# Row maxima and weight maxima of an attention kernel: over GpSimd and TensorE, or over VectorE's block transposes

## The chip, the core and the metric

The program runs on one core of a Trainium2 chip. The metric is the device time of one execution in microseconds, the median over several runs. Lower is better.

## The reference

A macaron block over x of shape 8 x 512 x 128 in float32: a feed-forward stage, an attention, and the same feed-forward stage again, each on a layer norm of x and added to x (the feed-forward stages with a factor 0.5).

```python
def attn(x, Q, K, VO):                                 # 16 heads, rank 64, dim 128
    xq = einsum('btd,hrd->bthr', x, Q)
    xk = einsum('bud,hrd->buhr', x, K)
    attn = softmax(einsum('bthr,buhr->bthu', xq, xk) / sqrt(128), axis=3)
    return einsum('bthu,bud,hde->bte', attn, x, VO)

def ffn(x):                                            # three blocks
    h = x
    for blk in range(3):
        y = qlora_linear(h, 2 * blk)                   # 4-bit weights, scales, bias, low-rank part
        y = gelu(layernorm(y, gamma[blk], beta[blk]))
        h = qlora_linear(y, 2 * blk + 1) + h
    return h

x = x + 0.5 * ffn(layernorm(x))
x = x + attn(layernorm(x), Q, K, VO)
x = x + 0.5 * ffn(layernorm(x))
```

## The kernel before, in words

Each engine has its own hand-written instruction stream, and the streams are tied by semaphores. There is no planner: the order on an engine is the order in the code.

**Feed-forward stage** (`ffn(f)` on each engine). Twelve units (three blocks of four units, a unit being two batches) go through a pipeline of steps i. On TensorE, step i holds the first linear layer of unit i (`lin1`, L899 and L902), the second of unit i - 3 (`lin2`, L919) and the turn of z of unit i - 2 (`turn_z`, L912). ScalarE makes squares (L441) and the gelu (L449); VectorE makes the seed of the reciprocal root (`seed`, L694 and L695), scales z (`z_scaled`, L703) and adds to h (`step_h`, L710); GpSimd runs three Newton steps of twelve small instructions on each unit's variances (`newton`, L333 to L336). Each batch has a PSUM bank of its own.

Beside the first of these stages the attention weights are prepared for a split into two fp16 halves. VectorE takes each partition's absolute maximum of Q, K and VO in steps 2, 3 and 5 and clamps it (`weight_maxima`, L616 to L621). After Newton step 5 GpSimd reduces these over all partitions with `partition_all_reduce` (L355). In step 7 VectorE makes powers of two and their inverses (`weight_scales`, L626 to L633). ScalarE makes the halves from step 7 on (`weight_halves`, L458 to L471), GpSimd the low halves after its last Newton step (L358, L360).

**Attention.** 128 heads (8 batches of 16) go through a pipeline of slots k, in a loop of four slots per turn, with the first and last ones written out. Heads are projected in pairs, since a head has 64 rows. What the engines do for head k or those near it in one slot:

- TensorE: scores of head k + 1 (`scores`, L986 and L987, eight matmuls of 512 columns); in even slots the turn of the row maxima of the pair k + 2, k + 3 (`turn_max`, L979); outputs of head k - 1 (`outputs`, L1008 to L1010, twelve of 128 columns); weighted sums of head k (`weigh`, L996 to L998, twelve of 512); a first product of queries and keys for the maxima of a pair ahead (`maxima`, L973, four of 512, 64 rows each); in odd slots the projections of queries and keys of a pair (`project`, L965 to L967, six of 512).
- ScalarE: exponentials of head k + 1 (`exps`, L522), their fp16 high half (`p_high`, L527), the high halves of a pair's queries and keys in odd slots (L514, L518), and the high half of y (L532).
- VectorE: in even slots the copy of the turned maxima of a pair into the score operands (`row_max`, L786); reciprocal and scaling of the outputs (`scale_out`, L795 and L799); two reductions of the maxima (`reduce_max`, L780, into `mcol`); in odd slots the low halves of queries and keys (L769, L774); the low half of y (`y_low`, L790).
- GpSimd: the low half of the exponentials (`p_low`, L375, two), and the addition of a head's output to x (L381).
- SyncE: ten DMAs per pair that spread the halves into `head_ops`, once the scores of the pair that used that place are done (`spread`, L260 to L271).

The row maximum reaches the scores as one more row of the product: row 64 or 96 of q2 holds minus the maximum, and the same row of k2 holds a one and zeros.

PSUM: banks 0 to 3 hold scores and maxima, bank 4 y, bank 5 the projected queries and, in other slots, the turned maxima, bank 7 the projected keys, and banks 6 and 7 the outputs, so that keys and outputs wait for each other.

Of the kernel before, what the change touches and what calls it, by code (L numbers as in the profile page):

```python
# [19 lines left out]
RMAX = bass.bass_isa.ReduceOp.max  # L20


def macaron(nc, x_d, q_d, k_d, vo_d, qw_d, sc_d, bias_d, la_d, lb_d, gam_d, bet_d, out_d):
# [14 lines left out]
    STEPS = NB * UNITS  # L38
    LN_EPS = 1e-5
# [7 lines left out]
    with ctx:  # L47
# [9 lines left out]
        ident16 = sb("ident16", [128, 128], F16)  # L57
# [22 lines left out]
        inv2 = sb("inv2", [128, 4])  # L80
        exp_scale = sb("exp_scale", [128, 1])
# [36 lines left out]
        mcol = sb("mcol", [128, 2, TT, 128], F16)  # L118
        M_ROWS = slice(R, R + 64, 32)
# [15 lines left out]
        qj_ps = ps[:, 5, :]  # L135
        kj_ps = ps[:, 7, :]
# [17 lines left out]
        prep_p = sem("prep_p")  # L154
        vo_folded = sem("vo_folded")
# [33 lines left out]
        m_turned = sem("m_turned")  # L189
# [13 lines left out]
        late_ps = ps[:, 6, :]  # L203

# [99 lines left out]
        def _(pool):  # L304
# [10 lines left out]
            pool.memset(mcol[:, :, :, :], 0.0).then_inc(prep_p, 1)  # L315
# [5 lines left out]
            pool.memset(head_ops[64:65, 0:RING:2, 3, :], 1.0).then_inc(prep_p, 1)  # L321
            pool.memset(head_ops[96:97, 1:RING:2, 3, :], 1.0).then_inc(prep_p, 1)
# [34 lines left out]
            pool.wait_ge(prep_p, 9)  # L357
# [54 lines left out]
        def _(act):  # L412
# [5 lines left out]
            nc.scalar.activation(ident_b[:, :], ident[:, :], ACT.Copy)  # L418
            nc.scalar.activation(ident16[:, :], ident[:, :], ACT.Copy).then_inc(prep_a, 1)
# [92 lines left out]
            def q_high(pair, buf):  # L512
                act.wait_ge(q_proj, pair + 1)
                nc.scalar.activation(pair_ops[:, buf, 0, :], qj_ps, ACT.Copy).then_inc(qh_ready, 1)  # L514

            def k_high(pair, buf):
                act.wait_ge(k_proj, pair + 1)
                nc.scalar.activation(pair_ops[:, buf, 2, :], kj_ps, ACT.Copy).then_inc(kh_ready, 1)  # L518
# [21 lines left out]
            def slot(k, j, lo, hi):  # L540
# [12 lines left out]
                if j % 2 == 1 and hi + 5 < NH:  # L553
                    turn = k // 4 if quad[0] is None else quad[0]
                    pair = 2 * turn + ((j + 5) // 2)
                    if lo + 5 >= 4:
                        pair_free(pair, ((j + 5) // 2) % 2, turn + (j + 5) // 4)
                    q_high(pair, ((j + 5) // 2) % 2)
                    k_high(pair, ((j + 5) // 2) % 2)
# [9 lines left out]
            for k in range(-5, 4):  # L569
# [25 lines left out]
        def _(dve):  # L595
# [130 lines left out]
            def ffn(f):  # L726
# [7 lines left out]
                for i in range(STEPS + 3):  # L734
                    if i >= 3 and i < STEPS + 2:
# [10 lines left out]
                    if f == 0 and i == 7:  # L746
                        weight_scales()
# [19 lines left out]
            def q_low(pair, buf):  # L767
                dve.wait_ge(qh_ready, pair + 1)
                nc.vector.tensor_tensor(pair_ops[:, buf, 1, :], qj_ps, pair_ops[:, buf, 0, :],  # L769
                                        ALU.subtract).then_inc(ql_ready, 1)  # L770

            def k_low(pair, buf):
                dve.wait_ge(kh_ready, pair + 1)
                nc.vector.tensor_tensor(pair_ops[:, buf, 3, :], kj_ps, pair_ops[:, buf, 2, :],  # L774
                                        ALU.subtract).then_inc(kl_ready, 1)

            def reduce_max(unit, par, t):

                dve.wait_ge(max_mm, unit + 1)
                nc.vector.tensor_reduce(mcol[:, par, t, M_ROWS], s_ps[t % 2], AX.X, ALU.max,  # L780
                                        negate=True).then_inc(max_red, 1)
# [20 lines left out]
            def slot(mine, i, k, j, lo, hi):  # L802
                if j % 2 == 0 and lo >= -2 and hi + 2 < NH:
                    row_max(2 * i + (j // 2 + 1), (j + 2) % 4)
# [7 lines left out]
                pair = 2 * i + (j + 5) // 2  # L812
                buf = ((j + 5) // 2) % 2
                if j % 2 == 1 and hi + 5 < NH:
                    if lo + 5 >= 4:
                        dve.wait_ge(spread_done[buf][0], 80 * (i + (j + 5) // 4))
                        dve.wait_ge(spread_done[buf][1], 80 * (i + (j + 5) // 4))
                    q_low(pair, buf)
                    k_low(pair, buf)
# [5 lines left out]
            for k in range(-5, 4):  # L825
# [34 lines left out]
        def _(pe):  # L860
# [53 lines left out]

            def lin2(f, i):
# [15 lines left out]
            def ffn(f):  # L931
# [5 lines left out]
                for i in range(STEPS + 3):  # L937
                    if i < STEPS:
                        lin1(f, i)
                    if i == 1:  # L940
                        pre(f, 1)
                    if i >= 3:
# [3 lines left out]
                    if 2 <= i < STEPS + 2:  # L946
                        turn_z(f, i - 2)
# [9 lines left out]
            pe.wait_ge(prep_p, 11)  # L957
# [18 lines left out]

            def turn_max(k, par):
                for t in range(TT):
# [153 lines left out]
```

## Time and profile before

| | us |
|---|---|
| median of 3 runs | 1062.44 (1061.88 to 1064.54) |
| profiled execution | 1065.14 |
| its span in the trace | 1063.3 |
| PE busy in the span | 992.4 (93%) |
| VectorE (DVE) busy | 806.0 (76%) |
| ScalarE (ACT) busy | 802.3 (75%) |
| GpSimd (POOL) busy | 785.8 (74%) |
| partition all-reduce, the instruction itself | 0.38 |

The profile shows one execution. Ends of matmuls are modelled, so the distance between the starts of matmuls says more than their length. A timeline row holds its start, its length, the engine, the line and the operation, and a row with "x4" stands for four instructions behind one another; in brackets stands how long the engine was idle before it and what ended that. In rows with "PEld" TensorE loads weights.

### The profile page before, as it was taken

The page shows a single profiled execution, that of the slowest core. Times are in us where ns is not written, and L with a number is a line of the kernel's source. Part 1 is how long each engine was busy: PE and PEld are TensorE (multiplying, and loading weights), DVE is VectorE, ACT ScalarE, POOL GpSimd, SP SyncE. Part 2 cuts the span into 40 slices and gives each one's busy share as a digit, 9 for nine tenths or more (in the row PEclk, how much of TensorE's full clock was granted, in tenths as well). Part 3 has the DMA queues.
Part 4 walks back from the last instruction along what each step waited for, and adds up shares of the span by engine and source line. Part 5 has one row for each costly group of instructions (what it writes and reads, how often), then busy time and mean ns, then how long its engine had stood idle before and what let it go on. Part 6 is the DMA issues. An engine that isn't in the chain of part 4 may idle for free.

```text
span 1063.3 us, 21754 instructions
## 1 busy us (share of the span) xinstructions
PE 992.4 (93%) x6145; PEld 515.5 (48%) x6145; DVE 806.0 (76%) x1335; ACT 802.3 (75%) x1294; POOL 785.8 (74%) x707
## 2 busy tenths in 40 slices
PE   4858578999999999999999999999999999997897
PEld 4736324444444444444444444444444444443775
DVE  7635887777777777777777777777777777778566
ACT  3847358788888888878888888788888888876874
POOL 3625237888888888888888888888888888887442
PEclk9978769999999999999999999999999999998899
DMA  9000021222222222222222222222222222220002
GB/s 235 2 0 1 20 70 41 64 62 62 63 63 62 59 59 59 59 59 59 59 59 59 62 62 64 63 62 62 63 63 62 59 59 59 59 60 1 1 2 80
DMA packets 71675, 59.02 MB, mean 56 GB/s; under 512 B 11168, under 2 KB 70560, under 8 KB 71648
## 3 DMA queue, kind: packets, MB, share of 16 engines
q1 hardware_dynamic: 71392, 58.31, 22.4%
q10 hardware_dynamic: 256, 0.39, 0.2%
q8 instruction: 12, 0.20, 0.1%
q14 instruction: 15, 0.12, 0.0%
HBM read 6.23 MB, written 2.10 MB: 8 GB/s over the span
## 4 chain that ended last, share of the span: by engine, by line
PE 84%; DVE 8%; ACT 3%; POOL 2%; issue 2%; DMA 1%; SPq 0%; DVEq 0%; POOLq 0%; ACTq 0%
PE ps L996 11%; PE ps L986 10%; PE ps L998 10%; PE ps L997 10%; PE ps L987 10%; PE ps L973 6%; PE ps L1009 3%; PE ps L965 3%; PE ps L1008 3%; PE ps L919 3%; PE ps L1010 3%; PE ps L967 3%; PE ps L966 3%; PE ps L902 2%; PE ps L979 1%
## 5 line engine op out<-in xcount | busy, mean ns | idle before, releaser
L375 POOL TENSOR_TENSOR p_lo<-work_b,p_hi 128x1024 f16<-128x1024 f32 x256 | 539.8, 2131 | 149.3 <-ACT p_hi L527 149.3
L780 DVE TENSOR_REDUCE mcol<-ps 128x2 f16<-128x1024 f32 x256 | 301.8, 1224 | 40.6 <-PE ps L973 40.5
L522 ACT ACTIVATE work_b<-ps,exp_scale 128x1024 f32<-128x1024 f32 x256 | 271.4, 1111 | 37.7 <-PE ps L987 37.4
L527 ACT ACTIVATE p_hi<-work_b 128x1024 f16<-128x1024 f32 x256 | 255.9, 1054 | 0.0
L986 PE MATMUL ps<-head_ops 128*128 128x512 f16 x512 | 195.3, 381 | 3.1 <-DVE mcol L780 1.7
L996 PE MATMUL ps<-p_hi,xn_hi 128*128 128x512 f16 x512 | 195.7, 382 | 0.0
L987 PE MATMUL ps<-head_ops 128*128 128x512 f16 x512 | 195.2, 381 | 0.0
L997 PE MATMUL ps<-p_hi,xn_lo 128*128 128x512 f16 x512 | 194.9, 381 | 0.0
L998 PE MATMUL ps<-p_lo,xn_hi 128*128 128x512 f16 x512 | 194.8, 380 | 0.0
L381 POOL TENSOR_TENSOR x<-x,o_sb 128x512 f32 (+1 forms) x128 | 163.1, 1274 | 10.4 <-DVE o_sb L799 10.4
L532 ACT ACTIVATE y_hi<-ps 128x512 f16<-128x512 f32 x128 | 76.5, 597 | 116.4 <-PE ps L998 116.2
L786 DVE CAST head_ops<-ps 64x1024 f16<-64x1024 f32 x64 | 78.6, 1227 | 37.2 <-PE ps L979 37.2
L1008 PE MATMUL ps<-vo_hi,y_hi 128*128 (+1 forms) x512 | 98.5, 222 | 6.9 <-DVE y_lo L790 6.9
L790 DVE TENSOR_TENSOR y_lo<-ps,y_hi 128x512 f16<-128x512 f32 x128 | 88.5, 691 | 14.6 <-ACT y_hi L532 8.8
L1009 PE MATMUL ps<-vo_lo,y_hi 128*128 (+1 forms) x512 | 94.4, 222 | 0.0
L1010 PE MATMUL ps<-vo_hi,y_lo 128*128 (+1 forms) x512 | 93.9, 221 | 0.0
L799 DVE TENSOR_TENSOR o_sb<-ps,rinv 128x512 f32<-128x512 f32 x128 | 88.4, 691 | 7.0
L986 PEld LDWEIGHTS ps<-head_ops 128*128 128x128 f16 x512 | 50.2, 98 | 73.6 <-DVE mcol L780 15.5
L973 PE MATMUL ps<-pair_ops 64*128 64x512 f16 x512 | 79.7, 387 | 5.1 <-ACT work_b L522 2.6
L795 DVE RECIPROCAL rinv<-ps 128x4 f32<-128x4 f32 x128 | 23.3, 182 | 76.7 <-PE ps L1010 74.7
L996 PEld LDWEIGHTS ps<-p_hi,xn_hi 128*128 (+1 forms) x512 | 50.2, 98 | 64.3 <-issue 27.1
L998 PEld LDWEIGHTS ps<-p_lo,xn_hi 128*128 (+1 forms) x512 | 50.3, 98 | 61.1 <-issue 1.1
(113 smaller groups left out, 1397.2 us busy)
## 6 DMA issues: line engine op xcount, KB each, us to landing
head_ops<-pair_ops SPq DMA_DIRECT2D x512, 64.0 KB, 2.0
head_ops<-pair_ops SPq DMA_DIRECT2D x128, 128.0 KB, 2.4
x<-x_dram SPq DMA_DIRECT2D x8, 256.0 KB, 6.4
out<-x SPq DMA_DIRECT2D x8, 256.0 KB, 3.0
vo_last<-wvo_dram SPq DMA_DIRECT2D x1, 1024.0 KB, 13.5
qk<-wq_dram SPq DMA_DIRECT2D x1, 512.0 KB, 5.3
qk<-wk_dram SPq DMA_DIRECT2D x1, 512.0 KB, 6.2
scl<-scales_dram ACTq DMA_DIRECT2D x8, 48.0 KB, 4.9
```

Source lines behind the costliest of these rows:

```text
L375: pool.tensor_tensor(p_lo[:, par, rows, :], p32[:, par, rows, :], p_hi[:, par, rows, :], ALU.subtract).then_inc(plo_done, 1)
L381: pool.tensor_tensor(rows, rows, o_sb[:, par, :, :], ALU.add).then_inc(x_added, 1)
L522: nc.scalar.activation(p32[:, par, 2 * a:2 * a + 2, :], s_ps[a], ACT.Exp, scale=exp_scale[:, 0:1]).then_inc(exp_done, 1)
L527: nc.scalar.activation(p_hi[:, par, 2 * a:2 * a + 2, :], p32[:, par, 2 * a:2 * a + 2, :], ACT.Copy).then_inc(phi_done, 1)
L780: nc.vector.tensor_reduce(mcol[:, par, t, M_ROWS], s_ps[t % 2], AX.X, ALU.max, negate=True).then_inc(max_red, 1)
L973: ins = nc.tensor.matmul(s_ps[t % 2][:, e, :], pair_ops[half, buf, 0, t * 128:(t + 1) * 128], pair_ops[half, buf, 2, :], start=True, stop= ...
L986: nc.tensor.matmul(s_ps[a][:, u % 2, :], k1[:, ring, keys], q1[:, ring, :], start=True, stop=False)
L987: ins = nc.tensor.matmul(s_ps[a][:, u % 2, :], k2[:, ring, keys], q2[:, ring, :], start=False, stop=True)
L996: nc.tensor.matmul(y_ps, xh, p_hi[:, par, u, :], start=(u == 0), stop=False)
L997: nc.tensor.matmul(y_ps, xl, p_hi[:, par, u, :], start=False, stop=False)
L998: ins = nc.tensor.matmul(y_ps, xh, p_lo[:, par, u, :], start=False, stop=(u == TT - 1))
L1008: nc.tensor.matmul(o, y_hi[:, cols], vh, start=True, stop=False)
```

## The change

Three things change.

1. **Weights' maximum.** `partition_all_reduce` goes from GpSimd's stream. In step 6 TensorE turns the three columns of maxima into three rows (`turn_tops`, ahead of `lin2` of unit 3), VectorE reduces them, takes the power of two and puts it on the diagonal of a 3x3 matrix (`weight_tops`, ahead of its `step_h`). In step 7 TensorE spreads the three values over the partitions with a matmul against a constant matrix (`spread_tops`), and VectorE copies them and makes the scales, now ahead of `step_h` (`weight_scales`). Banks 0 and 2 are borrowed, so the turns of z in steps 6 and 7 wait for VectorE.
2. **Row maxima.** `turn_max` and the copy of its result go. The reductions write columns 0 of blocks of 32 columns, and `row_max` runs for each head: four VectorE transposes of 32 x 32 blocks straight into rows 64 to 95 of that head's q2. The third matmul of `outputs`, not the first, waits for the low half of y.
3. **Projections.** Keys are projected in even slots, six ahead, and queries in odd ones, five ahead, both into bank 5. The attention begins with one more slot (k = -6). VectorE's low half of either comes after that of y.

```diff
-                if i == 5:
-                    pool.wait_ge(prep_v, 2)
-                    pool.partition_all_reduce(pow2[:, 0:3], amax[:, 0:3], 128, RMAX).then_inc(prep_p, 1)
...
+            def weight_tops():
+                dve.wait_ge(top_turned, 1)
+                link(dve, nc.vector.tensor_reduce(top[:, 0:1], top_rows, AX.X, ALU.max))
+                link(dve, nc.vector.tensor_scalar(top[:, 1:2].bitcast(I32), top[:, 0:1].bitcast(I32), EXPONENT, None,
+                                                  ALU.bitwise_and))
+                nc.vector.tensor_scalar(top_diag[:, 0:NTOP], ident[0:NTOP, 0:NTOP], top[:, 1:2], float(D), ALU.mult,
+                                        ALU.mult).then_inc(top_ready, 1)
...
             def weight_scales():
-                dve.wait_ge(prep_p, 9)
-                link(dve, nc.vector.tensor_scalar(pow2[:, 0:3].bitcast(I32), pow2[:, 0:3].bitcast(I32), EXPONENT,
-                                                  None, ALU.bitwise_and))
+                dve.wait_ge(top_spread, 1)
+                nc.vector.tensor_copy(pow2[:, 0:3], top_cols).then_inc(pow_ready, 1)
+                dve.wait_ge(pow_ready, 1)
...
+            def turn_tops(i):
+                pe.wait_ge(prep_v, 2)
+                pe.wait_ge(z_full, at(0, i, 0))
+                nc.tensor.transpose(top_rows, amax[:, 0:NTOP], ident[:, :]).then_inc(top_turned, 1)
+
+            def spread_tops(i):
+                pe.wait_ge(top_ready, 1)
+                pe.wait_ge(z_full, at(0, i, 0))
+                nc.tensor.matmul(top_cols, mean_mat[0:NTOP, :], top_diag[:, 0:NTOP], start=True,
+                                 stop=True).then_inc(top_spread, 1)
...
+                    if f == 0 and i == 6:
+                        turn_tops(i - 2)
+                    if f == 0 and i == 7:
+                        spread_tops(i - 2)
                     if i >= 3:
...
                         lin2(f, i - 3)
                     if 2 <= i < STEPS + 2:
+                        if f == 0 and i == 6:
+                            pe.wait_ge(top_ready, 1)
+                        if f == 0 and i == 7:
+                            pe.wait_ge(pow_ready, 1)
                         turn_z(f, i - 2)
...
-            def row_max(pair, ring):
-                dve.wait_ge(m_turned, pair + 1)
-                rows = qj_ps[64:128, :].rearrange("p (a t) -> p a t", a=1).to_broadcast([64, 2, T])
-                nc.vector.tensor_copy(q2[64:128, ring:ring + 2, :], rows).then_inc(m_ready, 1)
+            def row_max(k, pair, par, e, ring):
+                if not isinstance(k, int) or k >= 2:
+                    dve.wait_ge(s_done, 2 * k - 2)
+                dve.wait_ge(max_red, 4 * pair + 4)
+                for q in range(4):
+                    rows = q2[M_ROW, ring, :].rearrange("p (t c) -> p t c", c=128)
+                    ins = nc.vector.transpose(rows[:, :, 32 * q:32 * q + 32],
+                                              mcol[32 * q:32 * q + 32, par, e, :, :])
+                ins.then_inc(m_ready, 1)
...
-            def turn_max(k, par):
-                for t in range(TT):
-                    ins = nc.tensor.matmul(qj_ps[:, t * 128:(t + 1) * 128], mcol[:, par, t, :], ident16[:, :],
-                                           start=True, stop=True)
-                ins.then_inc(m_turned, 1)
...
-                    pe.wait_ge(m_ready, mine + 1)
+                    pe.wait_ge(m_ready, k + 2)
...
                 if lo >= 1:
-                    pe.wait_ge(yl_ready, k)
+                    pe.wait_ge(yh_ready, k)
                     if lo >= 2:
                         pe.wait_ge(o_scaled, k - 1)
-                    pe.wait_ge(kl_ready, projected(i, j))
...
+                ahead = 6 - j % 2
+                if hi + ahead < NH:
+                    pair = 2 * i + (j + ahead) // 2
+                    quads = i + (j + ahead) // 4
+                    pj_head = (quads % QPB) * 4 + (j + ahead) % 4
+                    if j % 2 == 0:
+                        if lo >= -4:
+                            pe.wait_ge(ql_ready, pair)
+                        project(pj_ps, 1, pj_head * R, quads // QPB, k_proj)
+                    else:
+                        pe.wait_ge(kl_ready, pair + 1)
+                        project(pj_ps, 0, pj_head * R, quads // QPB, q_proj)
```

## Rows read from the trace of the kernel before

**Rows 1.** One stretch: us, busy of PE, PEld, DVE, ACT, POOL; clock, DMA share, GB/s.

```profile
400.00:600.00 200.00, 200.00 (x1272) 94.72 (x1271) 157.92 (x203) 160.92 (x186) 167.83 (x94) 1.00 0.25 61
```

**Rows 2.** PE timeline of two slots: start us, us, engine, line, operation.

```profile
504.16 0.38 PE L986 MATMUL ps<-head_ops 128*128 128x512 f16 x1
...
505.89 0.39 PE L979 MATMUL ps<-ident,mcol 128*128 128x128 f16 x4
506.11 0.22 PE L1008 MATMUL ps<-vo_hi,y_hi 128*128 x1
...
510.02 0.38 PE L986 MATMUL ps<-head_ops 128*128 128x512 f16 x1
...
511.79 0.23 PE L1008 MATMUL ps<-vo_hi,y_hi 128*128 x1
511.92 0.23 PE L1009 MATMUL ps<-vo_lo,y_hi 128*128 x1
...
517.08 0.38 PE L986 MATMUL ps<-head_ops 128*128 128x512 f16 x1
```

**Rows 3.** GpSimd's timeline around the all-reduce; idle time before, in brackets.

```profile
61.45 0.38 POOL L355 PARTITION_ALL_REDUCE pow<-amax  x1 [5.64 <-issue]
68.81 0.19 POOL L333 TENSOR_TENSOR u_t<-u_rstd 128x8 f32<-128x8 f32 x1 [6.98 <-issue]
```

**Rows 4.** PE timeline, the second linear layers (L919) of the first feed-forward stage.

```profile
53.60 1.88 PE L919 MATMUL ps<-work_a,wt 128*128 128x512 f32 x4
...
59.06 1.88 PE L919 MATMUL ps<-work_a,wt 128*128 128x512 f32 x4
...
76.31 3.78 PE L919 MATMUL ps<-work_a,wt 128*128 128x512 f32 x4 [12.28 <-ACT work_a L449]
...
84.11 1.88 PE L919 MATMUL ps<-work_a,wt 128*128 128x512 f32 x4
...
88.92 1.88 PE L919 MATMUL ps<-work_a,wt 128*128 128x512 f32 x4
...
99.04 3.58 PE L919 MATMUL ps<-work_a,wt 128*128 128x512 f32 x4 [2.56 <-ACT work_a L449]
```

**Rows 5.** VectorE's timeline, the clamp of the weights' maxima.

```profile
55.96 0.17 DVE L621 TENSOR_SCALAR amax<-amax 128x3 f32<-128x3 f32 x1
```

**Rows 6.** VectorE's timeline of the same even slot as rows 2.

```profile
505.05 0.69 DVE L790 TENSOR_TENSOR y_lo<-ps,y_hi 128x512 f16<-128x512 f32 x1
506.31 1.23 DVE L786 CAST head_ops<-ps 64x1024 f16<-64x1024 f32 x1 [0.57 <-PE ps L979]
507.57 0.18 DVE L795 RECIPROCAL rinv<-ps 128x4 f32<-128x4 f32 x1
507.79 0.69 DVE L799 TENSOR_TENSOR o_sb<-ps,rinv 128x512 f32<-128x512 f32 x1
508.40 2.35 DVE L780 TENSOR_REDUCE mcol<-ps 128x2 f16<-128x1024 f32 x2
```

**Rows 7.** Timelines of GpSimd, then of VectorE, at the end of the attention.

```profile
959.51 4.22 POOL L375 TENSOR_TENSOR p_lo<-work_b,p_hi 128x1024 f16<-128x1024 f32 x2 [0.20 <-ACT p_hi L527]
...
969.10 1.27 POOL L381 TENSOR_TENSOR x<-x,o_sb 128x512 f32 x1
970.33 4.20 POOL L375 TENSOR_TENSOR p_lo<-work_b,p_hi 128x1024 f16<-128x1024 f32 x2
...
962.11 3.18 DVE L642 BATCH_NORM_STATS2 stats<-x 128x6 f32<-128x128 f32 x16
...
970.44 2.04 DVE L605 SCALAR_TENSOR_TENSOR rs_t<-rstd 128x16 f32<-128x16 f32 x1
...
974.80 0.17 DVE L605 SCALAR_TENSOR_TENSOR rs_t<-rstd 128x16 f32<-128x16 f32 x1
```

**Rows 8.** ScalarE's timeline, the exponentials of the same slot.

```profile
505.22 2.12 ACT L522 ACTIVATE work_b<-ps,exp_scale 128x1024 f32<-128x1024 f32 x2 [0.21 <-PE ps L987]
```

**Rows 9.** SyncE's queue, the last issue of the pair's spread.

```profile
511.76 0.60 SPq L271 DMA_DIRECT2D head_ops<-pair_ops  x1
```

More of the change, by code:

```diff
@@ L154, in macaron @@
         prep_p = sem("prep_p")
+        top_turned = sem("top_turned")
+        top_ready = sem("top_ready")
+        top_spread = sem("top_spread")
+        pow_ready = sem("pow_ready")
         vo_folded = sem("vo_folded")
@@ L552, in slot @@
                     p_high(k + 1, (j + 1) % 2, 1)
[L553 to L559, printed above, removed]
+                turn = k // 4 if quad[0] is None else quad[0]
+                ahead = 6 - j % 2
+                if hi + ahead < NH:
+                    pair = 2 * turn + (j + ahead) // 2
+                    if lo + ahead >= 4:
+                        pair_free(pair, ((j + ahead) // 2) % 2, turn + (j + ahead) // 4)
+                    if j % 2 == 0:
+                        k_high(pair, ((j + ahead) // 2) % 2)
+                    else:
+                        q_high(pair, ((j + ahead) // 2) % 2)
                 if 0 <= lo < SG:
@@ L567, in _ @@
             quad = [None]
-            for k in range(-5, 4):
+            for k in range(-6, 4):
                 slot(k, k % 4, k, k)
@@ L802, in slot @@
             def slot(mine, i, k, j, lo, hi):
-                if j % 2 == 0 and lo >= -2 and hi + 2 < NH:
-                    row_max(2 * i + (j // 2 + 1), (j + 2) % 4)
+                if lo >= -2 and hi + 2 < NH:
+                    row_max(k, 2 * i + (j + 2) // 2, (j + 2) // 2 % 2, j % 2, (j + 2) % 4)
                 if lo >= 1 and lo - 1 < NH:
@@ L823, in slot @@
                     y_low(k)
-            for k in range(-5, 4):
+                ahead = 6 - j % 2
+                if hi + ahead < NH:
+                    pair = 2 * i + (j + ahead) // 2
+                    buf = ((j + ahead) // 2) % 2
+                    if lo + ahead >= 4:
+                        dve.wait_ge(spread_done[buf][0], 80 * (i + (j + ahead) // 4))
+                        dve.wait_ge(spread_done[buf][1], 80 * (i + (j + ahead) // 4))
+                    if j % 2 == 0:
+                        k_low(pair, buf)
+                    else:
+                        q_low(pair, buf)
+            for k in range(-6, 4):
                 slot(link, k // 4, k, k % 4, k, k)
@@ L946, in ffn @@
                     if 2 <= i < STEPS + 2:
+                        if f == 0 and i == 6:
+                            pe.wait_ge(top_ready, 1)
+                        if f == 0 and i == 7:
+                            pe.wait_ge(pow_ready, 1)
                         turn_z(f, i - 2)
@@ L1000, in weigh, with outputs @@
                     ins.then_inc(av_half, 1)
-            def outputs(head):
+            def outputs(k, head):
                 vh = vo_hi[:, bass.ds(head, 1), 0:RW].rearrange("p a d -> p (a d)")
@@ L1028, in slot @@
                         scores(k + 1, (j + 1) % 4, a)
[L1029 to L1032 removed]
                 if lo >= 1:
[L1034 removed]
+                    pe.wait_ge(yh_ready, k)
                     if lo >= 2:
                         pe.wait_ge(o_scaled, k - 1)
[L1037 removed]
                     if hi < SG:
                         pe.wait_ge(xsplit_done, SG + k)
[L1040 removed]
+                    outputs(k, (4 * i + (j - 1)) % H)
                 if 0 <= lo < NH:
@@ L1057, in slot @@
                     weigh(j % 2, 1, i // QPB)
-                if j % 2 == 1 and hi + 5 < NH:
-                    if lo >= -1:
-                        pe.wait_ge(m_ready, ahead - 1)
-                    if lo >= -3:
-                        pe.wait_ge(ql_ready, ahead)
-                        pe.wait_ge(kl_ready, ahead)
-                    quads = i + (j + 5) // 4
-                    pj_head = (quads % QPB) * 4 + (j + 5) % 4
-                    project(qj_ps, 0, pj_head * R, quads // QPB, q_proj)
-                    if lo >= 1:
-                        pe.wait_ge(o_scaled, k)
-                    project(kj_ps, 1, pj_head * R, quads // QPB, k_proj)
+                ahead = 6 - j % 2
+                if hi + ahead < NH:
+                    pair = 2 * i + (j + ahead) // 2
+                    quads = i + (j + ahead) // 4
+                    pj_head = (quads % QPB) * 4 + (j + ahead) % 4
+                    if j % 2 == 0:
+                        if lo >= -4:
+                            pe.wait_ge(ql_ready, pair)
+                        project(pj_ps, 1, pj_head * R, quads // QPB, k_proj)
+                    else:
+                        pe.wait_ge(kl_ready, pair + 1)
+                        project(pj_ps, 0, pj_head * R, quads // QPB, q_proj)
                 if 0 <= lo < SG:
@@ L1077, in slot @@
                     weigh(j % 2, 3, i // QPB)
-            def projected(i, j):
-                n = 2 * i + (j // 2 + 3)
-                return n if not isinstance(n, int) else min(n, NH // 2)
-            for k in range(-5, 4):
+            for k in range(-6, 4):
                 slot(k // 4, k, k % 4, k, k)
```

58 lines of the change are left out of this document (22 added, 36 removed).

## The prediction

> **What bounds the kernel now.** I read the stretches of busy time first. [...] Two slots (two heads) take 517.08 - 504.16 = 12.92 us, the even one 5.86 and the odd one 7.06, because the odd one carries both projections. Eight 512-column matmuls take 1.73 us, so one takes 0.216. The four turns of the row maxima (L979) take 0.22. In the odd slot the output matmuls start at 511.79, 0.04 late, and the second follows 0.13 after the first, where 128 columns are worth 0.054 [rows 2].
>
> Then I looked at the stretch before the attention, where the engines show idle digits in the page. On GpSimd's timeline there is idle time of 5.64 us before the all-reduce over partitions, 0.38 us for the instruction itself, and 6.98 us behind it, both put down to issue: 13.0 us from 55.81 to 68.81 in which no Newton step runs [rows 3]. On TensorE the second linear layer of successive steps starts at 59.06, 76.31, 84.11 and 88.92 [rows 4]. The undisturbed step is 88.92 - 84.11 = 4.81 us. Counting back one such step from 84.11, the step after 59.06 is in effect at 79.30 instead of 63.87: 15.4 us lost. [...]
>
> **The change, part one: the weights' maximum.** [...] The 15.4 us come back, less what is put in. TensorE's turn of the maxima stands ahead of a second linear layer that started at 53.60 [rows 4], and waits for VectorE's clamp, which ends at 56.13 [rows 5]. That is a wait of 2.5 us, and everything behind it on TensorE is queued: that layer, the turns of z, the next first layer. Of this 0.65 was lost already (53.60 to 59.06 is 5.46, not 4.81), so it costs 1.9. The transpose, the three-row matmul, and VectorE's four new small instructions against one removed (0.17 us each, like the clamp) sit in steps that TensorE bounds. I take 0.3. The waits of the turns of z on the new results then fall behind a linear layer of 1.9 us and cost nothing. If that layer runs short they cost their chain, under 1 us. An idle time of 2.56 us before 99.04 was followed by a layer of 3.58 us instead of 1.88, at the lower clock [rows 4]. My wait is as long, so 0 to 1.7 more. ScalarE gets its scales after VectorE's, and its weight halves move up with the rest. Gain: 15.4 - 1.9 - 0.3 - 1.2 = **12 us**, bounds 9 and 14.
>
> **Part two: row maxima by VectorE.** TensorE loses the four turns per pair: 64 x 0.22 = 14.1 us. The output matmuls now wait at first only for y high, and for y low two matmuls later. VectorE's y low starts 0.89 after the slot's start and ends at 1.58 in the even slot [rows 2, 6]; in the odd one it was what made the outputs late. The third output matmul comes at 1.73 + 0.11, so its 0.04 + 0.08 goes: 64 x 0.12 = 7.7 at most, of which I take half, as the added wait may leave a gap of its own. Together **18 us**, bounds 13 (the pairs at both ends hide it) and 21.
>
> VectorE pays. It loses a copy of 1.26 us per pair (506.31 to 507.57) and gets eight transposes of 32 partitions x 128 elements. No such instruction is in the trace. From 512 elements at 0.69 and 1024 at 1.23 [rows 6] the slope is 1.05 ns an element on 0.15 us, so 128 elements are 0.285. The copy that writes other partitions than its follower is followed after 1.26, 0.03 more than its length; each transpose reads another block of 32 partitions, so I take 0.31 from start to start, 1.24 a head. The low end is 0.20, the pace of the batch-norm statistics over 128 elements (16 in 3.18 us) [rows 7]; the high end is 2.04, a VectorE instruction that waits for GpSimd (below). [...]
>
> VectorE's slot is then y low 0.6, one projection's low half 0.6, transposes 1.24, reciprocal and scaling 0.83 (507.57 to 508.40), two reductions 2.35 [rows 6]: 5.65 us, in a slot of 6.3 (12.92 - 0.22 - 0.1, halved). Starting from y low at 0.9, it ends the reductions near 6.6; TensorE's second half of scores overwrites that bank at 6.3 + 0.86 = 7.2. **The cover is 0.6 us**: costed at nothing, and gone from 0.46 us a transpose on.
>
> **Part three: alternate slots.** One bank takes keys in even and queries in odd slots. Each hand-over (project, high half, low half) ends about 2.2 into the next slot, and the next projection comes at 4.4: nothing. The slots become equal, 6.3 each, and the exponentials start 1.06 after the slot's start and last 2.12 [rows 2, 8], so to 3.18. TensorE reaches the maxima at 1.73 + 0.68 + 0.65 = 3.06 in the even slot, the second tile 0.3 later: about in time, at worst 0.1 a pair, 6 us, inside the bounds. SyncE's ten issues per pair keep their place behind the scores; the last is at 511.76, 7.6 us after the slot's start [rows 9]. The keys' high half of the pair that reuses the buffer comes at about 2 x 6.3 + 5.3 = 17.9. GpSimd's waits do not change.
>
> What the ends pay: the first pair's queries now wait until the keys' low half has been read, some 1.3 us longer, in a chain that VectorE bounds: -1 (bounds +1 and -4). In slots 1 to 3, where VectorE also normalises, 0.6 a slot: -1.5 (0 and -3). At the end the last head's transposes come behind the batch-norm statistics: -1 (+1 and -3).
>
> **Sum.** 12 + 18 - 1 - 1.5 - 1 = 26.5. The profiled execution took 1065.1 (span 1063.3 and 1.8 around it), 2.7 over the median of the three runs, 1062.4. 1065.1 - 26.5 = 1038.6, by the median **1036 us**. All bounds together give 1062.4 - 37 = 1025 and 1062.4 - 12 = 1050.
>
> **Rivals.** (a) *VectorE becomes the bound*, the one that ends slower. The transposes are the first steady VectorE instructions with source and destination both in SBUF. At 970.44 a tiny VectorE instruction with two SBUF inputs took 2.04 us, ending when GpSimd's subtraction of 970.33 was half way (one of its two instructions), and at 974.80 the same took 0.17 [rows 7]. If a transpose waits in that way behind GpSimd, even one wait of 1.27 us (GpSimd's add) makes the slot 5.65 + 1.27 = 6.9: 0.6 x 124 = 74 us, time **1110**. It decides from 0.46 us a transpose on. Against it: the statistics at 962.11, one SBUF input, kept 0.20 each beside a GpSimd subtraction that ran from 959.51 [rows 7]. [...]
> (b) *The steady gain does not come*: the added wait, the exponentials' 3.18 against 3.06 or VectorE's end of slot take back what the turns gave. Each is a few tenths a pair, and 0.25 x 64 = 16 would undo it. For it: three margins are under 0.6 us. Against: each was worked out positive. Time 1062.4 - 12 + 2 = **1052**.
> [...]
>
> **Chances.** Forecast 0.78, (a) 0.07, (b) 0.08, (c) 0.07. This kernel's measurement can tell about 0.3%, 3 us. Slower is (a); same is a bit of (b) with bad ends. Faster 0.91, same 0.02, slower 0.07. The range takes the forecast's bounds and (c), 1025 to 1050, leaving out (a) and (b).
>
> **What would show it.** Right: no gap on GpSimd between Newton steps, the granted clock at 1.00 or one short dip near 57 us; no L979 group; transposes near 0.3 us; slots of 6.3 us each, TensorE busy all through them; VectorE idle some 0.6 us a slot ahead of y low. Wrong: transposes over 0.46 us, TensorE's score matmuls waiting for the reductions or the row maxima, or a wait of several us around the new turn of the weights' maxima.

## The result, and the profile after

The changed kernel takes **1030.91 us** (median of 4 executions, 1026.52 to 1032.15), the kernel before 1062.91 on the same chip. The ratio is 0.9693, 95% interval 0.9665 to 0.9722, so 32.0 us less by the medians (29.5 to 35.6 by the interval); the prediction said 26.5 less. Its profiled execution took 1026.52, with a span of 1024.7. That is the fastest of its executions, while the profiled one of before, 1065.14, was slower than all others of its own, so the two spans differ by 38.6 and not by 32.

First the stretch of [rows 1] and three of VectorE's groups, from the page's list of the costliest groups (busy us, mean ns, idle us before, and its releaser).

```profile
400.00:600.00 200.00, 200.00 (x1242) 95.19 (x1240) 179.46 (x320) 165.55 (x192) 173.03 (x97) 1.00 0.27 62
```

```profile
L794 DVE TENSOR_REDUCE mcol<-ps 128x2 f16<-128x1024 f32 x256 | 301.0, 1220 | 0.8 <-PE ps L1015 0.7
...
L804 DVE STREAM_TRANSPOSE head_ops<-mcol 32x128 f16<-32x128 f16 x512 | 155.5, 304 | 9.3
...
L810 DVE TENSOR_TENSOR y_lo<-ps,y_hi 128x512 f16<-128x512 f32 x128 | 88.5, 691 | 60.5 <-ACT y_hi L532 60.4
```

TensorE is still busy for all of the 200 us at a granted clock of 1.00, as it was before [rows 1], so a slot is as long as its own stream. VectorE went from 158 to 179 us of 200 and is not the bound: in the attention its only idle time of any size, 60.5 us, lies ahead of the low half of y, where it waits for ScalarE.

The PE timeline of two slots answers to [rows 2]:

```profile
504.84 0.38 PE L1022 MATMUL ps<-head_ops 128*128 128x512 f16 x1
...
506.57 0.22 PE L1044 MATMUL ps<-vo_hi,y_hi 128*128 x1
506.63 0.22 PE L1045 MATMUL ps<-vo_lo,y_hi 128*128 x1
506.68 0.22 PE L1048 MATMUL ps<-vo_hi,y_lo 128*128 x1
...
511.13 0.38 PE L1022 MATMUL ps<-head_ops 128*128 128x512 f16 x1
...
517.42 0.38 PE L1022 MATMUL ps<-head_ops 128*128 128x512 f16 x1
```

Each slot takes 6.29 us, a pair 12.58 (12.57 to 12.58 over longer stretches, against 12.93). The turns are gone. The output matmuls start 1.73 after the slot's start and follow each other by 0.06, with no gap at the first, and none at the third, which now carries the wait for y low.

VectorE in one slot answers to [rows 6], and GpSimd beside it:

```profile
505.73 0.69 DVE L810 TENSOR_TENSOR y_lo<-ps,y_hi 128x512 f16<-128x512 f32 x1 [0.56 <-ACT y_hi L532]
506.34 0.68 DVE L783 TENSOR_TENSOR pair_ops<-ps,pair_ops 128x512 f16<-128x512 f32 x1
507.05 1.26 DVE L804 STREAM_TRANSPOSE head_ops<-mcol 32x128 f16<-32x128 f16 x4
508.34 0.18 DVE L815 RECIPROCAL rinv<-ps 128x4 f32<-128x4 f32 x1
508.56 0.69 DVE L819 TENSOR_TENSOR o_sb<-ps,rinv 128x512 f32<-128x512 f32 x1
509.17 2.35 DVE L794 TENSOR_REDUCE mcol<-ps 128x2 f16<-128x1024 f32 x2
512.02 0.69 DVE L810 TENSOR_TENSOR y_lo<-ps,y_hi 128x512 f16<-128x512 f32 x1 [0.50 <-ACT y_hi L532]
```

```profile
506.94 1.26 POOL L382 TENSOR_TENSOR x<-x,o_sb 128x512 f32 x1
509.05 4.22 POOL L376 TENSOR_TENSOR p_lo<-work_b,p_hi 128x1024 f16<-128x1024 f32 x2 [0.84 <-ACT p_hi L527]
```

Four transposes take 1.26 us and run from 507.05 to 508.31, exactly beside GpSimd's addition of 506.94 to 508.20. Neither is longer than elsewhere: a transpose takes 304 ns on average in this trace, the addition 1.27 us. VectorE's slot is 6.29 less the idle 0.50, so 5.79 us.

The first feed-forward stage, on TensorE, answers to [rows 4]:

```profile
54.82 0.27 PE L941 MATMUL ps<-ident,amax 128*3 128x128 f32 x1 [2.54 <-DVE amax L624]
54.93 1.88 PE L953 MATMUL ps<-work_a,wt 128*128 128x512 f32 x4
...
59.83 0.38 PE L946 MATMUL ps<-top_diag,mean_mat 3*128 3x3 f32 x2
60.13 1.98 PE L953 MATMUL ps<-work_a,wt 128*128 128x512 f32 x4
...
84.77 1.98 PE L953 MATMUL ps<-work_a,wt 128*128 128x512 f32 x4 [2.56 <-ACT work_a L449]
```

The wait for the clamp is there, 2.54 us against the 2.5 forecast, and so are no 12 us of idle time. GpSimd's longest pause between Newton steps is now 3.59:

```profile
58.02 0.20 POOL L338 TENSOR_TENSOR u_t<-u_rstd 128x8 f32<-128x8 f32 x1 [3.59 <-DVE u_rstd L707]
```

**Where the 38.6 us between the two spans lie**, counted by the starts of the same matmuls: 1.5 at the very start (the layers of the steps before the first edit acts already begin that much earlier); 12.8 up to the layer behind the old all-reduce; 1.7 where the layer that took 3.58 behind an idle 2.56 us [rows 4] now takes 1.98 behind the same idle time (granted clock 0.53 in that layer before, 1.00 now); back 1.5 between the first projection and the first scores; 0.3 from the scores of head 0 to those of head 4; 21.9 from head 4 to head 123; back 0.8 from there to head 127; 2.9 behind that (each rounded). Two of these are not the edits' alone. In the trace of parts two and three alone (below) heads 0 to 4 lose 0.9 instead of gaining 0.3, and only 2.0 come back behind head 127. There the second slot took 8.1 us at a granted clock of 0.80, where the changed kernel's took 6.7 at 1.00, and the 16 us from 20 us behind head 127's scores on ran at 0.79 instead of 0.89.

### The profile page after: what moved, and what is told of

Its sections match the earlier page's. It is cut to its first block, busy times and chain, and to the rows that moved or that the text cites. A ratio compares the mean times of both kernels' runs of the same rounds, so it can differ in the third digit from the quotient of the medians.

```text
span 1024.7 us, 22051 instructions
## 1 busy us (share of the span) xinstructions
PE 963.4 (94%) x5892; PEld 502.3 (49%) x5892; DVE 877.1 (86%) x1786; ACT 802.6 (78%) x1293; POOL 784.4 (77%) x706
## 4 chain that ended last, share of the span: by engine, by line
PE 83%; DVE 10%; ACT 3%; POOL 2%; issue 1%; DMA 1%; SPq 0%; DVEq 0%; POOLq 0%; ACTq 0%
PE ps L1032 11%; PE ps L1034 10%; PE ps L1033 10%; PE ps L1022 10%; PE ps L1023 10%; PE ps L1015 6%; PE ps L1007 3%; PE ps L953 3%; PE ps L1048 3%; PE ps L1044 3%; PE ps L1045 3%; PE ps L1009 3%; PE ps L1008 3%; PE ps L925 2%; DVE stats L654 1%
## 5 line engine op out<-in xcount | busy, mean ns | idle before, releaser
L804 DVE STREAM_TRANSPOSE head_ops<-mcol 32x128 f16<-32x128 f16 x512 | 155.5, 304 | 9.3
L810 DVE TENSOR_TENSOR y_lo<-ps,y_hi 128x512 f16<-128x512 f32 x128 | 88.5, 691 | 60.5 <-ACT y_hi L532 60.4
L1044 PE MATMUL ps<-vo_hi,y_hi 128*128 (+1 forms) x512 | 93.8, 221 | 5.6 <-DVE o_sb L819 5.6
L1022 PEld LDWEIGHTS ps<-head_ops 128*128 128x128 f16 x512 | 50.2, 98 | 68.8 <-issue 6.5
L1023 PEld LDWEIGHTS ps<-head_ops 128*128 128x128 f16 x512 | 50.2, 98 | 59.6 <-issue 0.8
```

The costliest lines, as they stand in the source:

```text
L804: ins = nc.vector.transpose(rows[:, :, 32 * q:32 * q + 32], mcol[32 * q:32 * q + 32, par, e, :, :])
L1022: nc.tensor.matmul(s_ps[a][:, u % 2, :], k1[:, ring, keys], q1[:, ring, :], start=True, stop=False)
L1023: ins = nc.tensor.matmul(s_ps[a][:, u % 2, :], k2[:, ring, keys], q2[:, ring, :], start=False, stop=True)
```

## The experiments

All times are medians of 4 to 6 executions. The kernel before was run beside each set: 1063.64 beside the first four kernels below, 1062.98 beside those with four more transposes and with one copy (on another chip), 1063.34 beside the other four.

### Part one alone

```diff
-                    pool.partition_all_reduce(pow2[:, 0:3], amax[:, 0:3], 128, RMAX).then_inc(prep_p, 1)
...
+                    if f == 0 and i == 6:
+                        turn_tops(i - 2)
+                    if f == 0 and i == 7:
+                        spread_tops(i - 2)
```
(with `weight_tops` and `weight_scales` as in the change; the attention as before)

> The kernel before with part one alone. My theory: the two profiled executions show the second linear layers 13.0 us closer (from the layer before the all-reduce to the first one at full pace) and 1.7 us more a little later, where the lower clock behind an idle 2.6 us does not show; so 13 to 15 us under the kernel before, about 1049. Rival: the steps after the feed-forward stage take it back, because VectorE bounds the first slots: under 8 us, about 1056. In the trace: GpSimd without a gap over 6 us between Newton steps, slots of the attention unchanged at 12.93 us a pair.

Measured: **1051.08**, ratio 0.9883 (0.9867 to 0.99), 12.6 less than before. A pair of slots takes 12.93, as before. That is a little under the 13 to 15 of this theory, and what the prediction had forecast for part one, 12.

### Parts two and three alone

```diff
+                if i == 5:
+                    pool.wait_ge(prep_v, 2)
+                    pool.partition_all_reduce(pow2[:, 0:3], amax[:, 0:3], 128, RMAX).then_inc(prep_p, 1)
```
(the changed kernel, with the weights' maximum made as before)

> The changed kernel with the all-reduce put back, so parts two and three alone. Theory: a pair of slots takes 12.58 us as in the changed kernel, 119 slots save 21.9, both ends together 0 to 2: 19 to 22 us under the kernel before, about 1042, and the sum of this gain and that of part one alone is that of the change, 32. Rival: the two parts share a gain (clock, first slots), and they sum to over 40 or under 26.

Measured: **1043.26**, ratio 0.9805 (0.9789 to 0.9821), 20.4 less than before; a pair takes 12.57. 12.6 and 20.4 are 33.0, against 32.0 for both: the parts add up, and neither lives on the other's wait.

### The wait for y low back in its place

```diff
-                    if t == 0:
-                        pe.wait_ge(yl_ready, k)
...
-                    pe.wait_ge(yh_ready, k)
+                    pe.wait_ge(yl_ready, k)
```

> The changed kernel, but the output matmuls wait for the low half of y ahead of the first of them, as before. Theory: low y ends 1.6 us into the slot, its arrival costs the first weight load, and two gaps of 0.04 and 0.08 us come back in most slots: 0.1 x 128 = 13 at most, 8 to 13 us over the changed kernel, about 1041; a pair takes 12.7 to 12.8. Rival: what went with the turns was the gap itself, as the equal slots give VectorE its time, and the wait's place is worth nothing: within 2 us of the changed kernel, a pair stays at 12.58.

Measured: **1047.43** (1042.86 to 1049.12), ratio 0.984 (0.981 to 0.987), 16.5 more than the changed kernel and over the theory's 8 to 13. PE timeline of one even slot:

```profile
503.51 0.38 PE L1023 MATMUL ps<-head_ops 128*128 128x512 f16 x1
503.87 0.23 PE L1044 MATMUL ps<-vo_hi,y_hi 128*128 x1
504.00 0.23 PE L1045 MATMUL ps<-vo_lo,y_hi 128*128 x1
504.06 0.22 PE L1046 MATMUL ps<-vo_hi,y_lo 128*128 x1
```

The first output matmul comes 0.36 behind the last score matmul instead of 0.22, and the second 0.13 behind the first instead of 0.06, 0.21 lost in this slot. VectorE's y low was ready at 503.58, 0.15 before the matmul's usual place (1.73 behind the slot's start at 502.00, so 503.73). What it was late for, by 0.06, is the usual place of that matmul's weight load. The loads in the changed kernel's slot of 504.84 and in this one:

```profile
506.36 0.10 PEld L1044 LDWEIGHTS ps<-vo_hi,y_hi 128*128 128x128 f16 x1
```

```profile
503.86 0.10 PEld L1044 LDWEIGHTS ps<-vo_hi,y_hi 128*128 128x128 f16 x1 [0.46 <-issue]
```

In the changed kernel the load runs 1.52 behind the slot's start, 0.21 ahead of its matmul and beside the last scores. With the old wait it runs at 1.86, right before its matmul. (Of the 0.28 from the end of y low to the load, no trace shows what they are.)

Over heads 10 to 110 a pair takes 12.85 instead of 12.58: 0.17 more in the even slot and 0.10 more in the odd one. The trace of before has the same wait, and there it costs 0.09 in the odd slot but only 0.05 in the even one, by the place of the last output matmul. In that even slot the turn of the maxima stood ahead of the outputs and covered most of the wait. So with the old wait the loss of the turns alone is worth 12.93 - 12.85 = 0.08 a pair, 5 us in all, and the move of the wait another 0.27, 17 us. Taken in the other order, by the trace of before, the move of the wait alone would be worth 0.05 + 0.09 = 0.14 a pair and the turns then their full 0.22 (an estimate; this was not run). Both orders end at the same 0.36, within rounding. (This kernel has the alternate slots too; the next experiment shows that they give nothing in the rhythm.)

### Both projections in odd slots again

```diff
-                ahead = 6 - j % 2
-                if hi + ahead < NH:
+                ahead = 5
+                if j % 2 == 1 and hi + ahead < NH:
...
+                    project(qj_ps, 0, pj_head * R, quads // QPB, q_proj)
+                    if lo >= 1:
+                        pe.wait_ge(o_scaled, k)
+                    project(kj_ps, 1, pj_head * R, quads // QPB, k_proj)
```
(the other engines alike: part three undone, parts one and two kept)

> The changed kernel with part three undone: both projections in odd slots, in banks 5 and 7, low halves ahead of the low half of y as before. Theory: TensorE's work is the same, VectorE's margin in the short even slot is still about 0.5 us, so a pair takes 12.6 us and the time is within 3 us of the changed kernel, about 1031. Rival: the even slot of 5.65 us is too short for VectorE with four transposes (5.1 us without low halves), or TensorE waits for the second maxima; then 0.2 to 0.5 us a pair, 13 to 32 us more, about 1045 to 1060.

Measured: **1027.94** (1026.91 to 1028.98), ratio 0.9661 (0.9645 to 0.9677). The slots are 5.64 and 6.93 us, the pair 12.57 as before this edit. Alternation gives nothing in the rhythm. Against the kernel before (5.91 and 7.02 on average) the even slot lost 0.27, which is the turns' 0.22 and 0.05 of the wait, and the odd one 0.09. The time is 3.0 lower than the changed kernel's. Its interval overlaps that of the changed kernel in the section on the result (0.9665 to 0.9722), but not that of its later measurement (0.9696 to 0.9723, below). All four executions had a mean granted clock of 0.979, where most of the changed kernel's had 0.974 to 0.976. Whether alternation itself costs these 3 to 4 us or the clock differed by chance is open.

### One more transpose, four more, and one copy

In all three the extra instructions write a spare tile, so the output is the same and only VectorE's slot grows. Ahead of them stands one more wait, of VectorE for its own transposes of the head before, which ended a slot earlier. The first of the three runs has it too and lost nothing by it.

```diff
+                if not isinstance(k, int) or k >= -1:
+                    dve.wait_ge(m_ready, k + 2)
+                nc.vector.transpose(spare[64:96, 0, :, :], mcol[0:32, par, e, :, :])
```

> The changed kernel with one more transpose per head, of the same form (32 x 128, fp16), into a spare tile, ahead of the four real ones. VectorE's slot grows by 0.31 us, and its margin ahead of the low half of y is 0.50. Theory (the price of a transpose decides only from the margin on, and the margin is real): the slots stay at 6.29, time as the changed kernel within 3 us, 1028 to 1034. Rival (the row maxima are already at their limit, as rival a of the prediction would have it): +0.31 a slot, 120 x 0.31 = 37 us, about 1068.

Measured: **1030.23** (1029.74 to 1031.37), 0.7 below the changed kernel. Slots from head 7 to head 120 are 6.29 us each, as without it. VectorE's idle time ahead of y low went on average from 0.48 to 0.29: the fifth transpose added only 0.19.

```diff
...
+                nc.vector.transpose(spare[64:96, 0, :, :], mcol[0:32, par, e, :, :])
+                nc.vector.transpose(spare[64:96, 1, :, :], mcol[32:64, par, e, :, :])
+                nc.vector.transpose(spare[64:96, 2, :, :], mcol[64:96, par, e, :, :])
+                nc.vector.transpose(spare[64:96, 3, :, :], mcol[96:128, par, e, :, :])
```

> The changed kernel with four more transposes per head into a spare tile, eight in all. VectorE's slot of 5.75 us grows by 1.25 to 7.0, over the 6.29 of TensorE. Theory (the prediction's threshold: cover 0.5 to 0.6 us a slot, then every further 0.1 is paid in full): slots of 6.9 to 7.0, 0.6 to 0.7 x 120 = 72 to 84 us more, about 1105 to 1115, TensorE waiting for the reductions or the row maxima in each slot. Rival (TensorE's rhythm has slack elsewhere, through the double buffers of mcol): under 40 us more.

Measured: **1118.85**, ratio 1.0532 (1.0515 to 1.055): 88 more than the changed kernel, somewhat over the theory's 72 to 84, and slower than before. Stretch and PE timeline of one slot:

```profile
400.00:600.00 200.00, 190.04 (x1114) 79.97 (x1112) 193.81 (x399) 151.66 (x172) 157.00 (x87) 1.00 0.25 58
```

```profile
507.09 0.39 PE L1029 MATMUL ps<-head_ops 128*128 128x512 f16 x1 [0.22 <-DVE mcol L795]
...
507.75 0.38 PE L1030 MATMUL ps<-head_ops 128*128 128x512 f16 x1
508.22 0.39 PE L1029 MATMUL ps<-head_ops 128*128 128x512 f16 x1
```

VectorE has no idle time left that another engine ends, and TensorE waits for its reductions ahead of both halves of the scores (0.22 idle, then 0.47 from matmul to matmul instead of 0.22). A slot takes 6.97 on average from head 7 to head 120: 0.69 more, by 120 slots 83 us. The rest of the 88 is at the ends. The eight transposes took 0.32 each from start to start. So the four more added 1.26 and 0.69 of it was paid: 0.57 a slot was free, close to the cover of 0.6 that the prediction worked out.

```diff
...
+                nc.vector.tensor_copy(spare[64:96, 0, :, :], mcol[64:96, par, e, :, :])
```

> The changed kernel with one fp16 tensor_copy of 32 x 128, SBUF to SBUF, per head into a spare tile, in the place of the one more transpose. By itself it is a short instruction, 0.1 to 0.3 us. Theory (a transpose is not held up by GpSimd because of its kind; a copy is, as the tiny instructions at the end of the attention were, by up to 2 us): the copy shows 1 to 2 us beside GpSimd's add or subtraction, the slot goes over the margin of 0.5, +0.5 a slot or more, time over 1080. Rival (a fp16 copy between SBUF places goes unhindered too): as the one more transpose, within 3 us of the changed kernel.

Measured: **1074.12** (1071.25 to 1075.4), ratio 1.0106 (1.0083 to 1.0128): 43 more than the changed kernel and 1.1% over the kernel before, where the transpose in the same place cost nothing. VectorE, then GpSimd:

```profile
505.32 1.06 DVE L805 COPY spare<-mcol 32x128 f16<-32x128 f16 x1
506.39 1.25 DVE L808 STREAM_TRANSPOSE head_ops<-mcol 32x128 f16<-32x128 f16 x4
...
512.08 0.73 DVE L805 COPY spare<-mcol 32x128 f16<-32x128 f16 x1
512.82 1.25 DVE L808 STREAM_TRANSPOSE head_ops<-mcol 32x128 f16<-32x128 f16 x4
```

```profile
505.06 1.27 POOL L383 TENSOR_TENSOR x<-x,o_sb 128x512 f32 x1
...
511.49 1.27 POOL L383 TENSOR_TENSOR x<-x,o_sb 128x512 f32 x1
```

GpSimd's additions end at 506.33 and 512.76, the copies at 506.38 and 512.81: each copy ends 0.05 behind the addition, whatever its own start. So do 124 of the 128 copies behind whatever GpSimd was running. The four that met no running instruction of GpSimd, at the start of the attention, took 0.19. The mean of the 128 copies is 861 ns. A slot takes 5.79 + 0.86 = 6.65 by that, and 6.64 on average in the trace. The theory's direction held, its size did not: the copy waits for the rest of the one addition, not for 1 to 2 us, and the time stayed under the 1080 that it named. By the two traces the copy took 861 ns on average and the one more transpose in its place 303. What makes the one wait and not the other, no trace shows.

### The weights' maxima one step later

```diff
-                    if f == 0 and i == 6:
+                    if f == 0 and i == 7:
                         turn_tops(i - 2)
-                    if f == 0 and i == 7:
+                    if f == 0 and i == 8:
                         spread_tops(i - 2)
...
-                        weight_halves(i)
+                        weight_halves(i - 1)
```
(banks 2 and 4 in place of 0 and 2; the waits of the turns of z and VectorE's part alike)

> The changed kernel with the turn of the weights' maxima, their spreading and the weight halves on ScalarE each one step later, in banks 2 and 4. The clamp ends long before TensorE comes to the turn. Theory (the idle 2.54 us ahead of the turn was TensorE's own loss, 1.9 us over the 0.65 that VectorE's reduction over VO costs anyway): the idle time goes, the step of 7.6 us becomes about 5.5, gain 1.9 to 2.2, time about 1029 by the medians. Rival (the wait only moves into the next step, or the halves of the weights come too late for the attention): same time as the changed kernel.

> The changed kernel itself, once more beside these variants, for the differences between them. 1031, within 0.3%.

Measured: **1026.96** (1024.37 to 1028.21), ratio 0.9655 (0.9638 to 0.9671), and the changed kernel in the same set **1031.61** (1026.38 to 1033.17), 0.971 (0.9696 to 0.9723). So 4.7 less. PE timeline:

```profile
55.55 0.39 PE L922 MATMUL ps<-bias_rows,ones_b 128*128 128x512 bf16 x1 [0.62 <-DVE hT L722]
...
57.78 0.27 PE L941 MATMUL ps<-ident,amax 128*3 128x128 f32 x1
57.89 1.88 PE L953 MATMUL ps<-work_a,wt 128*128 128x512 f32 x4
...
63.10 1.98 PE L953 MATMUL ps<-work_a,wt 128*128 128x512 f32 x4
```

The turn waits for nothing. The layer that began at 60.13 and the next at 65.04 now begin at 57.89 and 63.10, and the first projection at 107.95 instead of 110.16: 2.2 less, the theory's 1.9 to 2.2. The rest of the 4.7 goes with the clock (0.977 to 0.979 in the executions of this run). The profiled executions of the changed kernel, 1026.52 and 1026.38, are both the lowest of their sets. The others took 1030.4 to 1033.2, with a mean granted clock of 0.974 to 0.976 instead of 0.979. The kernel with one more transpose has the same instructions up to the attention, and its profiled execution (1031.37, clock 0.976) shows one stretch where such an execution loses time:

```profile
55.07 0.38 PE L945 MATMUL ps<-ident,amax 128*3 128x128 f32 x1 [2.62 <-DVE amax L625]
55.23 3.48 PE L957 MATMUL ps<-work_a,wt 128*128 128x512 f32 x4
...
62.04 1.98 PE L957 MATMUL ps<-work_a,wt 128*128 128x512 f32 x4
```

From layer to layer these are 6.81 us instead of 60.13 - 54.93 = 5.20, with a granted clock of 0.88 instead of 1.00 between 50 and 64 us. So the wait of 2.5 us has a second price, 1.6 us, in some executions: in two of the eight traces with that wait, this one and the one with the copy (idle 2.49). The two traces without the wait in that place do not have it. Against the execution above, the first projection of this run is 4.1 earlier. Two more places go with the clock in the same way: the second slot of the attention (6.7 us at 1.00, 8.0 to 8.1 at 0.79 or 0.80) and the end (1.0 us more at 0.79 than at 0.89). There the trace of this run has the lower values and those of the changed kernel the higher ones. How often each comes in the executions without a profile is not shown.

### All together

```diff
+                if hi == NH - 4:
+                    norm_stats(range(SG // 2))
                 if 0 <= lo and hi < NH:
                     y_low(k)
...
                 if k == NH - 4:
-                    norm_stats(range(SG))
+                    norm_stats(range(SG // 2, SG))
```
(on top of both projections in odd slots and of the weights' maxima one step later)

> Both projections in odd slots (part three undone), the weights' maxima one step later, and half of the batch-norm statistics of the attention's end moved into VectorE's idle 2.23 us of the slot before, so that the last row maxima come earlier. Theory: 0 to 3 from the first, 1.9 from the second, 1.0 to 1.6 from the third, together 3 to 6 under the changed kernel: 1025 to 1028. Rival: the three end in other waits, time as the changed kernel, 1031.

Measured: **1024.81** (1022.41 to 1025.7), ratio 0.9632 (0.9616 to 0.9648), 6.8 less than the changed kernel beside it, over the theory's 3 to 6, and faster than both kernels. The last row maxima came at 926.30, and the scores of head 127 came 5.00 behind those of head 126 instead of 6.02. But in the trace that 1.0 is given back directly:

```profile
930.76 1.10 DVE L603 TENSOR_SCALAR var<-mv 128x16 f32<-128x16 f32 x1
931.89 1.20 DVE L604 TENSOR_SCALAR rstd<-var 128x16 int32<-128x16 int32 x1
933.13 2.04 DVE L607 SCALAR_TENSOR_TENSOR rs_t<-rstd 128x16 f32<-128x16 f32 x1
935.21 2.04 DVE L608 TENSOR_TENSOR rs_u<-rs_t,var 128x16 f32<-128x16 f32 x1
937.28 0.17 DVE L609 SCALAR_TENSOR_TENSOR rstd<-rs_u,rstd 128x16 f32<-128x16 f32 x1
```

By their size these are instructions of 0.17 us. Each of the first four ended 0.03 to 0.04 behind one of GpSimd's, so they waited for it. In the changed kernel three did (1.19, 1.99, 2.04). From the scores of head 127 to the end are 95.8 us instead of 94.8, at the same granted clock (0.89 in the 16 us from 20 us behind those scores on). So the last of the three edits is not shown to be worth anything.

## Why the prediction was right, step by step

The time (1030.91 in 1025 to 1050) and the sign held, and none of the rivals came. But the sum was 26.5 where 32.0 was measured, and most of the 5.5 is in its second term.

- **Part one, 12 us:** 12.6 alone. That the 15.4 us go with the all-reduce was the prediction's estimate. The wait of 2.5 us was 2.54. Up to the layer behind the old all-reduce [rows 3, 4] the trace has 12.8 less, where 15.4 - 1.9 - 0.3 = 13.2 was counted. The 1.2 for a layer at the lower clock behind the wait was not paid in the profiled execution, but 1.6 was in that of the kernel with one more transpose. The term is real in some executions, and inside the 0 to 1.7 that the prediction gave it. No trace shows what GpSimd did in its idle 13 us, only that they went with the instruction. The lower clock is in the trace of before: a granted 0.50 in the layer of 3.78 us and 0.53 in that of 3.58 [rows 4]. Later in the stage it was even the other way round: the same idle 2.56 us was followed by 1.98, at a granted 1.00, instead of 3.58.
- **Part two, 18 us:** this is the mis-sized term. The pair went from 12.93 to 12.57, by 64 pairs 23 us, over the upper bound of 21. The step that failed is "64 x 0.12 = 7.7 at most, of which I take half, as the added wait may leave a gap of its own". The added wait left none, so nothing was to be halved. And the 0.12 were read in one odd slot: on average the old wait cost 0.09 in the odd and 0.05 in the even slot, 0.14 a pair, 9 us. With 14.1 for the turns that is the 23. So the mechanism held for the two edits together, and the size of its second half was a guess. What the prediction did not say is that the two prices hold only together. By the experiment with the wait in its old place, the turns alone are worth 0.08 a pair, 5 us. The turns of before had two uses: 0.22 of work, and the cover of a wait in the even slot. The prediction asked what covers the transposes; it did not ask what the removed matmuls had covered. Had the wait stayed first, its sum would have given 14.1 where 5 is found.
- **The transposes, 0.31 us, 1.24 a head:** 0.32 and 1.26. VectorE's slot was put at 5.65 (its terms add up to 5.62) and is 5.79; the idle time left is 0.50. One more transpose a head cost nothing, four more 88 us. The threshold of 0.46 us is a further 0.15 x 4 = 0.6 a head. The two runs bracket it, with 0.19 and 1.26 added, and by the 0.57 a slot that stayed free in the second it lies at 0.31 + 0.57 / 4 = 0.45 (an estimate).
- **Rival (a), VectorE becomes the bound:** its wait is real in this kernel and missed only the instruction. One more copy beside the transposes waited for GpSimd (861 ns on average, 0.19 us where GpSimd ran nothing) and made the whole slower than before (1074.12 against 1062.98), where one more transpose did not. Had the transposes waited as that copy did, 0.86 instead of 0.19 us, VectorE's slot would be 5.79 + 0.67 = 6.46, over the 6.29 of TensorE (an estimate).
- **Part three, 0:** 12.57 a pair with and without it. Whether the 3 to 4 us by which the kernel without it was faster are its price is open.
- **The ends, -3.5:** parts two and three alone gave 20.4 where 23 are in the rhythm, so about -2.5. In the trace that is 1.5 lost between projection and first scores, 0.8 at heads 123 to 127, with the transposes of head 127 behind the statistics as forecast. Behind head 127, 2.9 came back; 0.9 of it are small VectorE instructions that waited for GpSimd, three of them for 5.2 us in all against four for 6.2 before. About 0.9 more is the granted clock of that execution, 0.89 instead of 0.79; where parts two and three ran alone, 2.0 came back at 0.79, as in the kernel before. The rest was not followed. For slots 1 to 3 the prediction took 1.5, and 0.9 was lost between heads 0 and 4 in that trace.

## What to carry to other kernels

Before an instruction is taken out of a full engine's stream, look at what waited behind it: the wait that it covered comes to light in its place, and has to be moved too, or most of the gain is lost (here 0.08 of 0.36 us a pair was left). When work moves to an engine with slack, choose the instruction by its time beside the neighbours that it will have, not by its length alone: here one more 32 x 128 transpose a head was free and one more copy of that size, 0.19 us alone and 0.86 in its place, cost 43 us. And ask for a wait as late in a group of matmuls as its data allow (here two matmuls later was worth 16.5 us).

## What the runs showed of the hardware that was not expected

- The wait ahead of the first output matmul also held back its weight load. In the run with the wait for y low in its old place, data that were ready 0.15 us before the matmul's usual place made it 0.14 late in the slot shown, because the load, which otherwise ran 0.21 ahead of the matmul, ran right before it. The next matmul came 0.07 later than usual, 0.21 us in all. On the third matmul of the group, in the changed kernel, the same semaphore cost nothing: the matmuls start 0.05 to 0.06 apart, that one too.
- A fp16 copy of 32 x 128 within SBUF ended 0.05 us behind GpSimd's running instruction in 124 of 128 cases, also where it had started 0.6 after that, and took 0.19 in the four where GpSimd was idle. Transposes of the same tile ran beside the same addition at 304 ns in the changed kernel.
- The partition all-reduce showed 0.38 us of its own, and its removal with all that replaces it was worth 12.6 us of the whole.
- An idle time of TensorE of 2.56 us was followed by a layer of 3.58 us, at a granted clock of 0.53, in the kernel before [rows 4], and by one of 1.98 at 1.00 at the same place in the changed one. One of 2.54 was followed by no lower clock in the changed kernel (1.00 between 50 and 64 us), and one of 2.49 by a granted clock of 0.88 between 50 and 64 us in the kernel with the copy. So its length alone does not decide.
